# A two-layer attention kernel: softmax values and sums from one matrix product, quotients taken in transposed form

## The chip, the cores and the metric

The kernel runs on one core of one Trainium2 chip. The metric is device time in microseconds (us) of one execution. A core has a matrix engine (PE, TensorE), a vector engine (DVE), an activation engine (ACT), GpSimd (POOL) and DMA queues; most of the kernel's transfers are issued by SyncE (SP). PE writes only to PSUM, 8 banks of 2 KB in each of 128 partitions. Each engine executes its own instructions in program order and waits on semaphores that others raise.

## The reference, cut to what matters

Sixteen sequences of 256 tokens, model width 128, 16 heads of width 8, go through two layers, each `x = x + attention(norm(x)) * silu(feed_forward(norm(x)))`. The change touches attention alone:

```python
# layer 0 (full attention with a relative position bias)
scores = einsum('bhtd,bhsd->bhts', q, k) / sqrt(8) + rpe_bias
out = einsum('bhts,bhsd->bhtd', softmax(scores, -1), v)     # then heads side by side
s = out @ w_out + b_out

# layer 1 (causal)
attn = softmax(where(causal, q @ k.T / sqrt(8), -max), -1)
uniform = tril(ones / row)                                   # row = 1..256
new_attn = resid_gain * attn + skip_gain * eye - centre_gain * uniform
s = (new_attn @ v) @ cproj_w
```

The softmax of a row is computed as exponentials, their product with v ("values"), their sum ("sums"), and a quotient of the two.

## The kernel before

All is float32 but the scores' operands, which are split into three bfloat16 parts. Setup (to about 77 us) normalises, routes and builds tables; then comes attention of layer 0, the expert feed-forward and a middle part, and attention of layer 1. Expert and middle parts are not touched.

**Steps and units.** `attention()` is run once for each layer. Its work is a software pipeline over 16 batches (sequences): step k does pass A of batch k, pass B of batch k-1 and the end of batch k-2, and prepares q and k of batch k+1. Steps 3 to 14 are a hardware loop, the others are written out; layer 1's steps run from 0 to 17. Pass A computes scores with queries on the partitions and takes row maxima (DVE, L1178); pass B computes them transposed with the maximum subtracted, and takes exponentials (ACT, L1325 or L1330). A unit is 1024 columns of scores, that is two banks. There are 8 units a pass in layer 0 and 6 in layer 1, where the causal half is left out (units 0 to 3 have 256 columns a head, units 4 and 5 have 128). The class `Units` sets the order of a step, its positions numbered from 0:

```python
layer 0: A0 A1 A2 B0 A3 B1 A4 B2 A5 B3 A6 B4 A7 B5 B6 B7
layer 1: A0 A1 A2 B0 A3 B1 A4 B2 A5 B3 B4 B5
```

Six banks are a ring of three slots, one unit each: PE may write the unit at a position only when the unit three positions before has been read. In layer 0, DVE adds the position bias to each B unit (L1188) before ACT's exponential; in layer 1 ACT reads the ring itself.

**Values and sums.** `values()` (L1447) multiplies the exponentials of one unit by v: `vpad` holds v of each head in 8 of 32 columns, so that four heads fill the four 32-row strips of bank 6 (`od`), left half. In layer 0 the same routine then multiplies them by `onespad` for the sums, right half. In layer 1 POOL first adds units 4 and 5 onto units 0 to 3 (`add_tiles`, L1124), and PE takes sums of four units instead of six (`sums`, L1456). Units from `LATE` on (6 in layer 0, 2 in layer 1) are multiplied at the head of the next step, before A0 in layer 1 and after it in layer 0. `divide()` on DVE takes the reciprocal of the sums (L1198, 256 columns) and multiplies (L1203, L1205).

**Bank 7 (`misc`)** serves uses in a fixed order; `misc_free` makes each wait until the one before it in the list `MISC` has been read. They are QK (q and k of the next batch, L1464), V (v, L1487), in layer 1 E (the skip and centre products, L1493 and L1494), Y (output projection, L1503) and M (the maxima turned for pass B, L1517). `add_shape()` on DVE turns E into a running sum (L1213), weights it (L1216) and adds it to the quotient `on` (L1214, L1218). `project()` (L1244; L1249 and L1251) reads Y at the position `PROJECT`, the same at which PE computes Y.

**Operands of the scores.** ACT and POOL (in early steps of layer 0 DVE) split q and k (L1290 to L1301, L1111, L1116), SP writes the parts to DRAM (L1064) and loads them as `qs` and `ks` (L1071); A0 waits for these (16 x 2 loads of 384 KB).

## Time and profile before

| what | us |
|---|---|
| median of 3 runs | 1017.02 (1013.74 to 1020.98) |
| the profiled execution | 1019.83 |
| its span, first to last instruction | 1018.0 |
| PE busy | 853.4 (84%) |
| DVE busy | 729.1 (72%) |
| ACT busy | 455.0 (45%) |
| POOL busy | 336.7 (33%) |
| mean granted PE clock | 0.937 of full speed |

Layer 0's attention lies between about 78 and 490 us, layer 1's between about 717 us and the end. In a row of a timeline the first number is the start in us from the span's start, the second the time from the first start to the last end of `xcount` like instructions; a matrix product's row ends a little after the next one starts, because products are pipelined. A float32 product shows as two instructions. In brackets stands how long the engine had been idle and who released it.

### The profile page before, as it was taken

To read this page: it belongs to the slowest core of one execution; us is meant where nothing else is said; L and a number is where in the kernel's file an instruction comes from. 1 tells how busy PE (TensorE), PEld (TensorE's weight loads), DVE (VectorE), ACT (ScalarE), POOL (GpSimd) and SP (SyncE) were. 2 spreads that over 40 slices of the span, in tenths; PEclk is the share of its full clock that TensorE was granted. 3 is DMA by queue.
4 is the path that set the end of the run, shared out by engine and by line. 5 is a ranking of instruction groups with operands and counts; after the bars stand their busy time and mean duration, and the time that the engine had idled before them with its cause. 6 is when DMAs were issued, how large, how long until landed. Compare 5 with 4: busy or idle time off the path is not lost.

```text
span 1018.0 us, 21625 instructions
## 1 busy us (share of the span) xinstructions
PE 853.4 (84%) x7813; PEld 549.7 (54%) x7813; DVE 729.1 (72%) x1177; ACT 455.0 (45%) x809; POOL 336.7 (33%) x349
## 2 busy tenths in 40 slices
PE   0894785999999999999799999245689999999985
PEld 0742442555555555555366666234567666767763
DVE  5563784999999899997576767383557767676763
ACT  1252242454445444544344444277344545555532
POOL 7007773111111111100044444562135353434432
PEclk9996797999999999998799999757799999999999
DMA  5796441333332223223122222321543444444420
GB/s 138 227 156 162 118 110 34 79 74 73 85 68 63 63 63 78 63 48 126 33 67 66 67 67 66 101 83 46 110 100 87 109 95 102 87 110 94 99 44 11
DMA packets 105540, 88.37 MB, mean 87 GB/s; under 512 B 12565, under 2 KB 97497, under 8 KB 102409
## 3 DMA queue, kind: packets, MB, share of 16 engines
q1 hardware_dynamic: 96780, 76.54, 32.7%
q0 software_dynamic: 4352, 8.99, 2.9%
q10 hardware_dynamic: 4352, 2.10, 0.9%
q8 instruction: 35, 0.57, 0.2%
q14 instruction: 21, 0.17, 0.1%
HBM read 45.69 MB, written 41.11 MB: 85 GB/s over the span
## 4 chain that ended last, share of the span: by engine, by line
PE 19%; issue 13%; POOL 8%; DMA 4%; ACT 3%; DVE 3%; SPq 0%; POOLq 0%; ACTq 0%; DVEq 0%
PE ps L659 7%; POOL probs L1124 5%; PE ps L680 3%; DMA ks<-parts_d 3%; PE ps L661 2%; PE ps L671 2%; POOL qkr L1111 1%; POOL qk L1116 1%; ACT rows L875 1%; PE ps L653 1%; DMA parts_d<-qk 1%; PE ps L1398 1%; DMA probs<-mixed 1%; DVE mx L1178 0%; PE ps L912 0%
## 5 line engine op out<-in xcount | busy, mean ns | idle before, releaser
L1178 DVE TENSOR_REDUCE mx<-ps 128x4 f32<-128x1024 f32 (+1 forms) x224 | 269.9, 1218 | 100.4 <-PE ps L1398 67.3
L1325 ACT ACTIVATE probs<-probs 128x1024 f32<-128x1024 f32 x128 | 135.3, 1057 | 168.5 <-DVE probs L1188 166.0
L1188 DVE TENSOR_TENSOR probs<-ps,tabB 128x1024 f32<-128x1024 f32 x128 | 152.6, 1214 | 3.8 <-PE ps L1418 3.8
L1330 ACT ACTIVATE probs<-ps 128x1024 f32<-128x1024 f32 x96 | 96.5, 1023 | 97.0 <-PE ps L1456 39.4
L1447 PE MATMUL ps<-probs,vpad 128*32 128x256 f32 (+1 forms) x2048 | 131.6, 363 | 3.2 <-ACT probs L1325 1.2
L1390 PE MATMUL ps<-tabA,eyeb 128*128 128x512 bf16 x256 | 100.6, 393 | 29.8 <-DVE probs L1188 18.0
L1124 POOL TENSOR_TENSOR probs<-probs 128x512 f32<-128x512 f32 x64 | 78.9, 1264 | 136.1 <-PE ps L1447 136.1
L747 POOL DMA_INDIRECT mixed<-probs x72 | 69.7, 968 | 112.3 <-DVE probs L736 111.7
L1392 PE MATMUL ps<-ks,qs 96*128 96x256 bf16 x512 | 100.4, 277 | 0.0
L1418 PE MATMUL ps<-qs,ks 99*128 99x256 bf16 x512 | 76.2, 278 | 16.8 <-DVE mx L1178 11.4
L1198 DVE RECIPROCAL rden<-ps 128x256 f32<-128x256 f32 x32 | 56.2, 1756 | 36.5 <-PE ps L1456 24.8
L1447 PE MATMUL ps<-probs,onespad 128*32 128x256 f32 x1024 | 81.5, 391 | 0.0
L659 PE MATMUL ps<-qs,probs 128*128 x144 | 80.0, 638 | 0.0
L1447 PEld LDWEIGHTS ps<-probs,vpad 128*32 128x32 f32 x2048 | 53.5, 110 | 47.7 <-issue 17.9
L1111 POOL TENSOR_TENSOR qkr<-qkf,qk 128x512 f32<-128x512 f32 x28 | 32.3, 1154 | 126.7 <-ACT qk L1297 126.7
L1392 PEld LDWEIGHTS ps<-ks,qs 96*128 96x128 bf16 x512 | 51.5, 100 | 36.8 <-issue 3.6
L1152 POOL DMA_INDIRECT slots_in<-rows,place x64 | 62.3, 973 | 19.6 <-issue 18.9
L1418 PEld LDWEIGHTS ps<-qs,ks 99*128 99x128 bf16 x512 | 45.2, 98 | 42.2 <-DVE mx L1178 26.9
L718 DVE TENSOR_SCALAR probs<-ps 128x256 f32<-128x256 f32 x72 | 30.6, 425 | 49.5 <-PE ps L661 49.5
L700 ACT ACTIVATE probs<-ps 128x256 f32<-128x256 f32 x72 | 27.7, 385 | 78.9 <-PE ps L671 78.9
L1116 POOL TENSOR_TENSOR qk<-qkr,qk 128x512 bf16<-128x512 f32 x28 | 32.3, 1154 | 80.9 <-ACT qk L1301 80.9
L1390 PEld LDWEIGHTS ps<-tabA,eyeb 128*128 128x128 bf16 x256 | 25.7, 100 | 49.4 <-DVE probs L1188 26.4
(225 smaller groups left out, 1578.6 us busy)
## 6 DMA issues: line engine op xcount, KB each, us to landing
parts_d<-qk SPq DMA_DIRECT2D x64, 192.0 KB, 2.3
qs<-parts_d SPq DMA_DIRECT2D x32, 384.0 KB, 4.9
ks<-parts_d SPq DMA_DIRECT2D x32, 384.0 KB, 6.7
parts_d<-qk SPq DMA_DIRECT2D x64, 128.0 KB, 1.9
slots_in<-probs SPq DMA_DIRECT2D x1, 4680.0 KB
probs<-slots_in SPq DMA_DIRECT2D x72, 65.0 KB, 1.8
parts_d<-qk SPq DMA_DIRECT2D x64, 64.0 KB, 1.6
probs<-mixed SPq DMA_DIRECT2D x16, 256.0 KB, 3.3
```

The costliest lines, as they stand in the source:

```text
L659: nc.tensor.matmul(ps[:, b, :], xgT[:, b, :], wgu[:, bass.ds(e, 1), :].rearrange("p a n -> p (a n)"), start=True, stop=False)
L747: nc.gpsimd.indirect_dma_start(v.mixed[:, :], bass.IndirectOffsetOnAxis(ap=rows[:, b:b + 1], axis=0), yo[:, b % 4, :], None).then_inc(y_st ...
L1124: nc.gpsimd.tensor_tensor(later, later, second, ALU.add).then_inc(added, 1)
L1152: nc.gpsimd.indirect_dma_start(v.slots_in[:, :], bass.IndirectOffsetOnAxis(ap=v.place[:, k, t:t + 1], axis=0), v.rows[:, t, :], None).then ...
L1178: nc.vector.tensor_reduce(mx[:, s.buf(), t, heads[0]:heads[-1] + 1], ring[:, slot].rearrange("p (h n) -> p h n", n=w), AX.X, ALU.max).then ...
L1188: nc.vector.tensor_tensor(probs[:, j, :].rearrange("p (h n) -> p h n", n=T), ring[:, slot].rearrange("p (h n) -> p h n", n=T), v.tabB[:, h ...
L1325: nc.scalar.activation(probs[:, j, :], probs[:, j, :], ACT.Exp).then_inc(exp_done, 1)
L1330: nc.scalar.activation(probs[:, j, :], ring[:, slot], ACT.Exp).then_inc(exp_done, 1)
L1390: nc.tensor.matmul(o[:, T * n:T * n + 2 * T], eyeb[:], v.tabA[:, h:h + 2, off:off + T], start=True, stop=False, skip_group_check=True)
L1392: mm = nc.tensor.matmul(at, q, ks[0:MROW, b, h, :], start=False, stop=True, skip_group_check=True)
L1418: mm = nc.tensor.matmul(at, k, qs[0:MROW + PARTS, b, h, :], start=(n % 2 == 0), stop=True, skip_group_check=True)
L1447: mm = nc.tensor.matmul(od[32 * q:32 * q + 32, T * what + t0:T * what + T], lhs, probs[:, j, w * n:w * n + w], start=(j == 0 and what == 0 ...
```

## The change

Values and sums come from one product: `vpad` now has v in 8 columns, ones in the next 8 and zeros in 16, and a head's 32 columns are taken from a place that puts values and sums of two groups of heads above each other in a strip, in the left or right half of `od`. `add_tiles` and `sums` are gone, and so is `onespad`. At position 0 of a step (layer 1) or 1 (layer 0) ACT copies `od` to SBUF (`copy_products`), PE turns it so that tokens are on the partitions (`tokens_apart`, use T of bank 7), DVE takes reciprocals of 32 columns and multiplies (`divide`), and PE turns the result back (`heads_apart`, use N): in layer 0 by two transposes and a copy by ACT (`quotients`, at position `BACK`), in layer 1 by adding it as a product into the bank that holds the skip product. The residual gain moves into v's weights. The order of bank 7 becomes QK, T, N, Y, V, M. The diff, with setup's edits cut:

```diff
-        v.vpad = sb("vpad", [P, 3, 8, 160])
-        v.onespad = sb("onespad", [P, 4, 32])
+        v.vpad = sb("vpad", [P, 3, 8, 128])
...
     LATE = 2 if layer else 6
-    PROJECT = 10 if layer else 11
-    GROUPS = 4
+    APART, DIVIDE, BACK, PROJECT, VALUE = (3, 2, 6, 8, 10) if layer else (4, 5, 7, 9, 12)
+    PROJECTED = PROJECT + 1
...
-    MISC = ["QK", "V", "E", "Y", "M"] if layer else ["QK", "V", "Y", "M"]
+    MISC = ["QK", "T", "N", "Y", "V", "M"]
...
             def divide(s):
-                if layer == 0:
-                    dve.wait_ge(pv_done, NU * (s.n(-2) + 1))
-                else:
-                    dve.wait_ge(sum_done, GROUPS * (s.n(-2) + 1))
-                nc.vector.reciprocal(rden[:], od[:, T:2 * T]).then_inc(rd_done, 1)
+                dve.wait_ge(apart_full, s.n(-2) + 1)
...
+                turned = misc.rearrange("p (g e d) -> p g e d", e=2, d=HD)
+                nc.vector.reciprocal(rden[:], turned[:, :, 1, 0]).then_inc(rd_done, 1)
                 dve.wait_ge(rd_done, s.n(-2) + 1)
...
+                nc.vector.tensor_tensor(onT[:].rearrange("p (g d) -> p g d", d=HD), turned[:, :, 0, :],
+                                        rden[:].unsqueeze(2).broadcast_to([P, 2 * H, HD]), ALU.mult).then_inc(apart_done, 1)
+
+            def add_shape(s):
+                n = 2 * s.n(-2)
+                dve.wait_ge(e_full, s.n(-2) + 1)
+                nc.vector.tensor_tensor_scan(cum[:], v.onesT[:], misc[:, T:2 * T], 0.0, ALU.mult, ALU.add).then_inc(e_evac, 1)
+                dve.wait_ge(e_evac, n + 1)
+                nc.vector.tensor_tensor(cum[:], cum[:], v.share, ALU.mult).then_inc(shaped, 1)
+                dve.wait_ge(shaped, s.n(-2) + 1)
...
+                nc.vector.tensor_tensor(on[:], misc[:, 0:T], cum[:], ALU.add).then_inc(e_evac, 1)
...
                 for pos, (kind, j) in enumerate(U.order):
-                    if layer == 0 and pos == 1 and s.has(-2):
+                    if pos == DIVIDE and s.has(-2):
                         divide(s)
                     if U.exists(s.k, kind):
                         (maximum if kind == "A" else add_bias if layer == 0 else lambda *a: None)(s, j, U.slot(s.k, pos))
                     if kind == "A" and j == NU - 1 and s.has() and (layer or s.k < LOOP):
                         maximum_parts(s)
-                    if layer and pos == 4 and s.has(-2):
-                        divide(s)
-                    if layer and pos == 7 and s.has(-2):
+                    if layer and pos == BACK and s.has(-2):
                         add_shape(s)
...
-                    if pos == PROJECT and s.has(-2):
+                    if pos == PROJECTED and s.has(-2):
                         project(s)
...
+            def copy_products(s):
+                act.wait_ge(pv_done, NU * (s.n(-2) + 1))
...
+                nc.scalar.activation(ods[:].rearrange("p r t -> p (r t)"), od, ACT.Copy).then_inc(od_copied, 1)
+
+            def quotients(s):
+                act.wait_ge(back_full, s.n(-2) + 1)
...
+                nc.scalar.activation(on[:], misc[:, 0:T], ACT.Copy).then_inc(on_done, 1)
...
-                for what in range(2 if layer == 0 else 1):
-                    for n, h in enumerate(heads):
-                        i, q = h // 4, h % 4
-                        lhs = vpad[:, b, 4 * c + q, 32 * i:32 * i + 32] if what == 0 else onespad[:, i, :]
-                        mm = nc.tensor.matmul(od[32 * q:32 * q + 32, T * what + t0:T * what + T], lhs,
...
+                for n, h in enumerate(heads):
+                    i, q = h // 4, h % 4
+                    r, first_column = i % 2, 32 * i - 16 * (i // 2)
+                    mm = nc.tensor.matmul(od[32 * q:32 * q + 32, T * r + t0:T * r + T],
+                                          vpad[:, b, 4 * c + q, first_column:first_column + 32],
...
+            def tokens_apart(s):
+                misc_free(pe, s, "T")
+                pe.wait_ge(od_copied, s.n(-2) + 1)
+                for c in range(2):
+                    for r in range(2):
+                        at = 2 * P * c + P * r
+                        mm = nc.tensor.transpose(misc[:, at:at + P], ods[:, r, P * c:P * c + P], eye)
+                mm.then_inc(apart_full, 1)
+
+            def heads_apart(s):
+                misc_free(pe, s, "N")
+                if layer == 0:
+                    pe.wait_ge(apart_done, s.n(-2) + 1)
+                    for c in range(2):
+                        mm = nc.tensor.transpose(misc[:, P * c:P * c + P], onT[:, P * c:P * c + P], eye)
+                    mm.then_inc(back_full, 1)
+                else:
+                    nc.tensor.matmul(misc[:, T:2 * T], v.wv1[:, 1, :], batch_tokens(s, -2), start=True, stop=True,
+                                     skip_group_check=True)
+                    nc.tensor.matmul(misc[:, 0:T], v.wvs[:], batch_tokens(s, -2), start=False, stop=False, skip_group_check=True)
+                    pe.wait_ge(apart_done, s.n(-2) + 1)
+                    for c in range(2):
+                        mm = nc.tensor.matmul(misc[:, P * c:P * c + P], onT[:, P * c:P * c + P], eye, start=False, stop=True,
+                                              skip_group_check=True)
+                    mm.then_inc(e_full, 1)
...
+                    if pos == PROJECT and s.has(-2):
+                        misc_free(pe, s, "Y")
+                        if layer:
+                            pe.wait_ge(e_evac, 2 * (s.n(-2) + 1))
+                        else:
+                            pe.wait_ge(on_done, s.n(-2) + 1)
...
-                    if pos == 4 and s.has():
+                    if pos == VALUE and s.has():
                         misc_free(pe, s, "V")
```

What this does to the order of PE in layer 1 (a step of the hardware loop; `wo,on` is the output projection Y, `maskA` and `ks,qs` with 128x512 and 128x128 are unit A5 or A4, `maskB` with 128x2x128 is a B unit, `probs,vpad` are values 0 and 1). Before:

```order
L1401 MATMUL ps<-maskA,eyeb 128x512
L1403 MATMUL ps<-ks,qs 128x128 x4
L1401 MATMUL ps<-maskA,eyeb 128x512
L1403 MATMUL ps<-ks,qs 128x128 x4
L1374 REGISTER_ALU
L1422 MATMUL ps<-maskB,eyeb 128x2x128
L1424 MATMUL ps<-qs,ks 128x256 x2
L1422 MATMUL ps<-maskB,eyeb 128x2x128
L1424 MATMUL ps<-qs,ks 128x256 x2
L1447 MATMUL ps<-probs,vpad 32x256 x8
L1503 MATMUL ps<-wo,on 128x128 x2
L1427 MATMUL ps<-maskB,eyeb 128x512
```

This is A5, B3, values 0 and 1, and only then Y. With the change the same engine has, from A4 on:

```order
L1413 MATMUL ps<-maskA,eyeb 128x512
L1415 MATMUL ps<-ks,qs 128x128 x4
L1413 MATMUL ps<-maskA,eyeb 128x512
L1415 MATMUL ps<-ks,qs 128x128 x4
L1386 REGISTER_ALU
L1434 MATMUL ps<-maskB,eyeb 128x2x128
L1436 MATMUL ps<-qs,ks 128x256 x2
L1434 MATMUL ps<-maskB,eyeb 128x2x128
L1436 MATMUL ps<-qs,ks 128x256 x2
L1525 MATMUL ps<-wo,on 128x128 x2
L1413 MATMUL ps<-maskA,eyeb 128x512
L1415 MATMUL ps<-ks,qs 128x128 x4
```

Y now stands behind A4 and B2 and ahead of A5. On DVE in layer 1, `add_shape` of before, between the maxima of A4 and A5:

```order
L1178 TENSOR_REDUCE mx<-ps 128x8 [waits l1_a_full]
L1213 SCALAR_TENSOR_TENSOR cum<-onesT,ps 128x256 [waits l1_on,l1_e_full]
L1214 TENSOR_TENSOR on<-ps,on 128x256
L1215 ISA
L1216 TENSOR_TENSOR cum<-cum,cst 128x256 [waits l1_e_evac]
L1217 REGISTER_ALU
L1218 TENSOR_TENSOR on<-on,cum 128x256 [waits l1_shaped]
```

and the same place with the change:

```order
L1179 TENSOR_REDUCE mx<-ps 128x8 [waits l1_a_full]
L1208 SCALAR_TENSOR_TENSOR cum<-onesT,ps 128x256 [waits l1_e_full]
L1209 ISA
L1210 TENSOR_TENSOR cum<-cum,cst 128x256 [waits l1_e_evac]
L1214 TENSOR_TENSOR on<-ps,cum 128x256 [waits l1_y_full,l1_shaped]
```

One addition is gone; the group still stands behind the maximum of A4. On DVE in layer 0, the head of a step before (B5 to B7, A0, divide, A1, A2, B0):

```order
L1188 TENSOR_TENSOR probs<-ps,tabB 128x1024 [waits l0_pv_done,l0_b_full] x3
L1177 ISA
L1178 TENSOR_REDUCE mx<-ps 128x4 [waits l0_a_full]
L1198 RECIPROCAL rden<-ps 128x256 [waits l0_pv_done]
L1203 TENSOR_TENSOR on<-ps,rden 128x256 [waits l0_y_full,l0_rd]
L1177 REGISTER_ALU
L1178 TENSOR_REDUCE mx<-ps 128x4 [waits l0_a_full]
```

and with the change (A0, A1, A2, B0, A3, divide, B1):

```order
L1179 TENSOR_REDUCE mx<-ps 128x4 [waits l0_a_full]
L1178 REGISTER_ALU
L1179 TENSOR_REDUCE mx<-ps 128x4 [waits l0_a_full]
L1178 REGISTER_ALU
L1179 TENSOR_REDUCE mx<-ps 128x4 [waits l0_a_full]
L1189 TENSOR_TENSOR probs<-ps,tabB 128x1024 [waits l0_pv_done,l0_b_full]
L1178 REGISTER_ALU
L1179 TENSOR_REDUCE mx<-ps 128x4 [waits l0_a_full]
L1199 RECIPROCAL rden<-ps 128x32 [waits l0_back_full,l0_apart_full]
L1201 TENSOR_TENSOR onT<-ps,rden 128x256 [waits l0_rd]
L1189 TENSOR_TENSOR probs<-ps,tabB 128x1024 [waits l0_pv_done,l0_b_full]
```

The division has moved from behind A0 to behind A3.

## Rows read from the trace of the kernel before

**Rows 1.** Timeline of DVE, layer 0, one step from A0's maximum on

```profile
240.74 1.23 DVE L1178 TENSOR_REDUCE mx<-ps 128x4 f32<-128x1024 f32 x1 [1.05 <-PE ps L1392]
242.63 1.76 DVE L1198 RECIPROCAL rden<-ps 128x256 f32<-128x256 f32 x1 [0.67 <-PE ps L1447]
...
244.86 2.35 DVE L1178 TENSOR_REDUCE mx<-ps 128x4 f32<-128x1024 f32 x2
...
263.54 1.22 DVE L1178 TENSOR_REDUCE mx<-ps 128x4 f32<-128x1024 f32 x1 [1.05 <-PE ps L1392]
```

**Rows 2.** Timelines of PE and ACT at the head of that step

```profile
242.50 1.13 PE L1464 MATMUL ps<-xnT,wqk 128*128 x4
243.46 0.38 PE L1390 MATMUL ps<-tabA,eyeb 128*128 128x512 bf16 x1
...
237.46 3.32 ACT L1325 ACTIVATE probs<-probs 128x1024 f32<-128x1024 f32 x3 [1.54 <-DVE probs L1188]
```

**Rows 3.** Timeline of PE, layer 1, one step from A0 to the next A0

```profile
886.81 0.28 PE L1396 MATMUL ps<-maskA,eyeb 128*128 128x256 bf16 x1 [0.35 <-DMA ks<-parts_d]
...
887.49 1.03 PE L1464 MATMUL ps<-xnT,wqk 128*128 x4
...
890.34 0.61 PE L1487 MATMUL ps<-wv,xb 128*128 128x128 f32 x4
...
891.54 1.93 PE L1456 MATMUL ps<-probs,onespad 128*32 128x256 f32 x32
...
894.08 0.38 PE L1401 MATMUL ps<-maskA,eyeb 128*128 128x512 bf16 x1
...
894.97 0.65 PE L1493 MATMUL ps<-xnT,wvs 128*128 x2
...
904.03 0.28 PE L1396 MATMUL ps<-maskA,eyeb 128*128 128x256 bf16 x1 [0.43 <-DMA ks<-parts_d]
```

**Rows 4.** Lines of layer 1's division over the whole trace: DVE timeline, first and eleventh

```profile
752.85 1.76 DVE L1198 RECIPROCAL rden<-ps 128x256 f32<-128x256 f32 x1 [0.67 <-PE ps L1456]
...
928.08 1.76 DVE L1198 RECIPROCAL rden<-ps 128x256 f32<-128x256 f32 x1 [0.67 <-PE ps L1456]
```

**Rows 5.** Small operations of the kinds added: reciprocal (DVE, setup), transposes (PE, experts)

```profile
75.89 0.35 DVE L339 RECIPROCAL wt<-probs 128x32 f32<-128x32 f32 x1
...
561.75 0.38 PE L671 MATMUL ps<-cst,probs 128*128 128x128 f32 x2
```

**Rows 6.** Timeline of DVE in the step of rows 3: `add_shape`, maxima's parts, `project`

```profile
896.87 0.68 DVE L1213 TENSOR_TENSOR_SCAN cum<-onesT,ps 128x256 f32<-128x256 f32 x1
...
897.89 0.42 DVE L1216 TENSOR_TENSOR cum<-cum,cst 128x256 f32<-128x256 f32 x1
898.35 0.42 DVE L1218 TENSOR_TENSOR on<-on,cum 128x256 f32<-128x256 f32 x1
...
899.94 0.18 DVE L1227 CAST m<-mx 128x32 bf16<-128x32 f32 x1
...
900.80 0.42 DVE L1249 TENSOR_TENSOR yt<-ps,rows 128x256 f32<-128x256 f32 x1
```

**Rows 7.** Last step of layer 1: timelines of PE (values, first sums) and DVE

```profile
1002.34 1.94 PE L1447 MATMUL ps<-probs,vpad 128*32 128x256 f32 x48
1005.27 0.64 PE L1456 MATMUL ps<-probs,onespad 128*32 128x256 f32 x8 [0.99 <-POOL probs L1124]
...
1012.04 0.69 DVE L1213 TENSOR_TENSOR_SCAN cum<-onesT,ps 128x256 f32<-128x256 f32 x1
```

**Rows 8.** Early step of layer 1: PE timeline; windows (busy per engine, granted clock 0.67, DMA)

```profile
744.46 0.28 PE L1396 MATMUL ps<-maskA,eyeb 128*128 128x256 bf16 x1 [2.00 <-DMA ks<-parts_d]
...
749.64 0.61 PE L1487 MATMUL ps<-wv,xb 128*128 128x128 f32 x4
...
744.40:747.80 3.40, 3.34 (x17) 2.46 (x18) 1.22 (x1) 1.07 (x3) 2.66 (x3) 0.67 0.00 0
```

**Rows 9.** Timeline of POOL, layer 1, the step of rows 3: the last part of q and k

```profile
893.87 1.15 POOL L1116 TENSOR_TENSOR qk<-qkr,qk 128x512 bf16<-128x512 f32 x1 [1.67 <-ACT qk L1301]
```

More of the change, by code:

```diff
@@ L65 @@
 C_ALL = C_SPARE + FLIGHT
-W_LOADS, R_LOADS = 14, 5
+W_LOADS, R_LOADS = 16, 5
 PAIR_OF_MINUS_ONES = float.fromhex("-0x1.017f00p+0")
@@ L522, in _ @@
                     mm.then_inc(lg, 1)
-            pe.wait_ge(copied, 4 + 4 + 13)
-            for k in range(6):
+            pe.wait_ge(copied, 4 + 4 + 15)
+            for k in range(5):
                 nc.tensor.matmul(ps[:, 2, k:k + 1], rowsp[:, k, :], v.ones[0:1, 0:1], start=True, stop=True)
@@ L1157, in body @@
             def body(s):
-                if layer and s.has(-2):
-                    for g in range(GROUPS):
-                        add_tiles(pool, s, g)
                 if s.has(1) and (layer or s.k >= LOOP):
@@ L1346, in body @@
                 for pos, (kind, j) in enumerate(U.order):
+                    if pos == (0 if layer else 1) and s.has(-2):
+                        copy_products(s)
+                    if layer == 0 and pos == BACK and s.has(-2):
+                        quotients(s)
+                    if pos == VALUE and s.has():
+                        values(s)
                     if kind == "B" and U.exists(s.k, kind):
@@ L1450, in values @@
-                mm.then_inc(pv_done, 1)
-            def sums(s, g):
-                pe.wait_ge(added, GROUPS * s.n(-2) + g + 1)
-                for q in range(4):
-                    mm = nc.tensor.matmul(od[32 * q:32 * q + 32, T:2 * T], onespad[:, g, :], probs[:, g, T * q:T * q + T],
-                                          start=False, stop=(g == GROUPS - 1), skip_group_check=True)
-                mm.then_inc(sum_done, 1)
+                for n, h in enumerate(heads):
[3 more added lines that the diff above has]
+                                          vpad[:, b, 4 * c + q, first_column:first_column + 32],
+                                          probs[:, j, w * n:w * n + w], start=(j == 0 and i == 0),
+                                          stop=(j == NU - 1), skip_group_check=True)
@@ L1481, in body @@
                         projections(s)
-                    if pos == 4 and s.has():
+                    if pos == APART and s.has(-2):
+                        tokens_apart(s)
+                    if pos == BACK and s.has(-2):
+                        heads_apart(s)
+                    if pos == PROJECT and s.has(-2):
[4 more added lines that the diff above has]
+                            pe.wait_ge(on_done, s.n(-2) + 1)
+                        for c in range(2):
+                            mm = nc.tensor.matmul(misc[:, D * c:D * c + D], on[:, P * c:P * c + P], wo[:],
+                                                  start=True, stop=True)
+                        mm.then_inc(y_full, 1)
+                    if pos == VALUE and s.has():
                         misc_free(pe, s, "V")
@@ L1510, in body @@
                         values(s, -1, j - 2)
-                    if layer and pos == 4 and s.has(-2):
-                        for g in range(GROUPS):
-                            sums(s, g)
                 if s.has():
```

117 lines of the change are left out of this document (47 added, 70 removed).

## The prediction

> **What bounds the kernel now.** I read first the busy times, which name PE, and then one steady step of each layer in the timelines, since the two layers have different limits.
>
> In layer 0 a step takes 22.80 us, from one maximum of A0 to the next [rows 1]. Sixteen passes of DVE over 1024 columns (two of them start 1.13 apart: 2.35 us for both) make 18.1 of these. The division takes 2.23, from 242.63 to 244.86, and the projection's addition some 0.35. The rest, about 2.1, is waiting, most of it at the step's head: 1.05 before A0's maximum and 0.67 before the division. So DVE bounds layer 0, and the head of a step, where PE and ACT finish the batch before, adds to it.
>
> In layer 1 a step is 17.22 us from A0 to A0 [rows 3], on the mean of ten steps 17.52 ((928.08 - 752.85) / 10) [rows 4]. PE is idle in it for 0.43 us only, before A0, and waits there for the load of `ks`. So layer 1 is bound by PE, with the way of q and k through DRAM just behind: from the end of POOL's last part at 895.02 [rows 9] to A0 at 904.03 it is 9.0 us. In these rows a product's entry runs 0.16 past the start of the next, and the engine that reads it starts 0.2 after that start; I use 0.2 for each handover from PE and 0.05 for the others.
>
> **Layer 1, what is saved.** The sums cost PE 1.9 us a step [rows 3]; they go, and values and sums come at the price of values alone, as the same 32 columns are loaded and the same columns streamed. POOL's additions go as well, so the parts of q and k are ready earlier. Added to PE: four transposes of 128 columns and two float32 products of 128. The transposes: two took 0.38 with 0.16 of overlap, so 0.11 each and 0.45 for four [rows 5]. The products: V is the same pair, 0.61 - 0.16 = 0.45 [rows 3]. PE's work is 17.22 - 0.43 = 16.8 before and 16.8 - 1.9 + 0.45 + 0.45 = 15.8 after. If nothing else waited, a step would gain 1 us.
>
> The Trainium skill (TensorE: Matmul & The Clock Gate, Part 4: PE-mode transpose) gives about 275 ns for a 128x128 transpose in one kernel's context. By it four would take 1.1 and not 0.45, and a step 0.65 more. The row shows 0.38 for two, so back to back they are cheaper, and the sum goes by the row.
>
> **Layer 1, what waits.** The new positions put three waits on PE, which executes in order. I follow a step from A0 = 0, with 0.68 for a unit of 256-column heads (886.81 to 887.49), 0.86 for QK and 0.89 for A4 and A5 (894.08 to 894.97) [rows 3].
>
> 1. B1 writes the slot of A2. `divide` now stands on DVE ahead of A2's maximum. PE: A0 to 0.68, QK to 1.54, A1 and A2 to 2.9, transposes to 3.35, B0 and A3 to 4.7. DVE: A1's maximum 2.4 to 3.55, reciprocal of 32 columns 0.35 (setup has this very shape [rows 5], where 256 columns took 1.76), product 0.42 [rows 6], A2's maximum from 4.3 on, finished at 5.5. PE waits 0.85.
> 2. Y is computed at position 8 and needs `on`. Behind the end of A4's product comes 0.2, its maximum 1.13, the scan 0.68, then 0.03, the weighting 0.42, 0.04, the last addition 0.42 and 0.05 [rows 6]: 2.97 in all. PE has only B2 in between, 0.67. It waits 2.3. Before, Y stood behind A5, B3 and values 0 and 1 as well, which covered the same chain. Behind the waiting Y stands everything: A5, B3, the values; DVE itself runs dry, since A5's maximum is its next work.
> 3. V is at position 10 and its bank is free when `project` has read Y. DVE gets there from Y's start after Y 0.45, A5 0.89, 0.2, A5's maximum 1.25, the four operations on the maxima 0.86 (899.94 to 900.80), the product and its signal 0.47 [rows 6]: 4.1. PE has Y, A5, B3 and values 0 and 1 (half of what four sums cost, 0.95, with a gap of 0.1): 3.1. It waits 1.0.
>
> A step is then 15.8 + 0.85 + 2.3 + 1.0 = 19.95, against 17.52 on the mean, 2.45 more. Steps 2 to 15 have all three parts: 14 x 2.45 = +34. ACT's new copy (512 columns, 0.6 as about half an exponential over 1024, three of which take 3.32 [rows 2]) lies beside A0 and QK and is done 2 us before the transposes; without that cover each 0.1 would cost as much. The load of `ks` is no longer late: q and k are ready at about 7 (B0's product 4.0, exponential 1.1, ACT's part 0.6, POOL's 1.15), plus 9.0 is 16, and A0 comes at 19.9.
>
> **Layer 1, its end.** The last step has no units. Before, from the end of the values at 1004.28 to the scan at 1012.04 it was 7.75 us, with PE waiting for POOL's additions [rows 7]. Now the way is copy 0.2 + 0.6, transposes 0.15 + 0.45, reciprocal and product 0.2 + 0.8, skip and centre products with the quotients 0.05 + 1.35, and 0.2: 4.0. With one addition less behind the scan (0.35) this gives -4.1. Step 16 has no A units either and loses part of its wait for POOL: -1.3. Together -5.4.
>
> **Layer 0.** At the head, unit 5's values and sums take 0.45 less, so A0's maximum can begin at 240.3. The three last exponentials end at 240.78 all the same [rows 2], because DVE's additions feed them; then values 7 (0.05 + 0.45), QK 0.96 (242.50 to 243.46), A1 0.89 (as many columns as A4 of layer 1) and 0.2 bring A1's maximum to 243.3, where it was 244.86: -1.55. The long reciprocal had stood in this gap and was largely covered by it. The new division costs DVE 0.75 in the middle, where DVE has no gap. V at position 12 waits for the projection's addition behind A6 and then delays A7: project's start + 0.4 + V 0.45 + A7 0.89 + 0.2 is 1.9, while DVE has 1.45 of work: +0.5. Net -0.3 to -0.2 a step, 13 steps: -3. In step 2 the projection's addition also waits until POOL's scatter for the expert part has landed; it now has one more B unit behind it, +1.1, one pass of DVE [rows 1]. Together -2. The reciprocal's 1.4 us a step thus brings almost nothing.
>
> **The clock.** In an early step PE had been idle for 2.00 us, and the next stretch has a mean granted clock of 0.67, that is in part the lower level of 1.2 GHz [rows 8]. From A0 to V it took 5.18 us there (744.46 to 749.64) and 3.53 in the steady step (886.81 to 890.34) [rows 3]: 1.65 lost. The wait at Y is longer than that 2.00, but it is followed by work that is partly covered by the wait at V. I count half of the 14 steps at 1.0: +7, with bounds of 0 and 14 x 1.65 = 23.
>
> **The sum**, against the profiled execution's own 1019.8: +34 - 5.4 - 2 + 7 = +33.6, so 1053.4. Setup changes by a few short operations beside idle stretches, under 0.5. The profiled execution is 2.8 above the median of the runs shown; against the median the sum gives 1050.6. I forecast 1052.
>
> Bounds: the three waits may be each off by 0.2 or 0.3 from handovers, -0.7 to +0.7 a step, -10 to +10. A transpose by the row of a product pair rather than back to back (0.38 for two without overlap) gives +0.3 a step, +4. The product with the broadcast reciprocal has no row; it lies between 0.35 and 1.22 (DVE's pass over 1024 columns), and I take 0.42, the row of 256 columns; at the upper end +0.8 on the first wait and in each step of layer 0, +20, which no row supports.
>
> **Rivals.**
> *The clock falls in every step* (0.16). For it: each step now has a wait longer than that of [rows 8], and the other two beside it. Against: it has more work around it. 14 x 1.65 instead of 7 gives +16: 1068. Beside it stands the Trainium skill (the same page, A second HAM failure mode: psum-queue depth-cycling), which reports a clock that oscillates with frequent short idle times of PE; no steady step shows that here, the clock in these stays at 2.4 GHz with PE waits of 0.4.
> *Layer 0 gains its head in full* (0.12): A7 is not delayed and the new division falls into a gap. Then 13 x 1.3 more: 1038.
> *Layer 0 loses* (0.08): PE does some 3 us less there in about the same step, in short pieces, and the clock falls there too, 13 x 1: 1065.
> *The other side, not slower* (0.06): the wait at Y does not arise, because DVE's chain behind A4 is done before PE has written B2. Then V's wait shrinks too, and the way of q and k decides: 7 + 9.0 = 16.0 a step, 14 x -1.5 = -21, and with the end and layer 0 about 992. It turns at one number: A4's product to the last addition must take less than 0.67, where the rows add up to 2.97. It could come about only if DVE had no maximum to take first.
>
> **How the numbers follow.** The forecast's own case has 0.58, the rivals 0.16, 0.12, 0.08 and 0.06. Its own range is 1041 to 1064. For 8 in 10 I reach down to the full gain of layer 0 and up to the clock in every step: 1036 to 1072. Faster by over 1% (about what a measurement of this kernel can tell from none): the last rival, 0.05. Within 1%: what lies between it and the rest, 0.04. Slower by over 1%: 0.91.
>
> **What would show it.** In layer 1's steady step: PE idle before Y by about 2.3 with DVE as releaser, before V by about 1.0, before B1 by 0.85; no wait for `ks`; a period near 20. In layer 0: a DVE wait of about 1.9 before A1's maximum, about 0.5 before A7's, a period near 22.6. In the last step 4 us from values to scan. I am wrong if layer 1's period is under 18.5 or PE does not wait at Y; only mis-sized if the waits are there and the clock differs.

## The result, and the profile after

| | before | after |
|---|---|---|
| median of the runs | 1017.99 us (1013.74 to 1020.98, 4 runs) | 1055.18 us (1051.31 to 1063.01, 4 runs) |
| profiled execution: time, span | 1019.8, 1018.0 us | 1051.31, 1049.5 us |
| ratio of the times | 1 | 1.0378, 95% interval 1.0304 to 1.0453 |

The change makes the kernel 37 us slower; 1052 was forecast, with a range of 1036 to 1072. The busy times of the page for the kernel after:

```profile
PE 805.7 (77%) x6484; PEld 531.1 (51%) x6499; DVE 681.6 (65%) x1164; ACT 479.3 (46%) x857; POOL 258.8 (25%) x282
```

No engine is close to full, and yet the kernel is slower: waits were added, not work. Below are the waits of PE from 720 us on: which products waited and for what, then the us in total, how often, and the longest. Before, PE waited in most steps of layer 1 only for `ks`, 0.4 in the step of [rows 3] and 1.3 at most between 760 and 1000 us.

```profile
PE ps L1525 <- DVE on L1214: 34.5, 16, 2.3
PE ps L1533 <- DVE yt L1245: 12.5, 14, 1.0
PE ps L1434 <- DVE mx L1179: 11.1, 14, 1.0
PE ps L1408 <- DMA ks<-parts_d: 2.2, 1, 2.2
```

L1525 is the projection Y, L1533 the value projection V, L1434 the first product of B1. The load of `ks` makes PE wait once, in an early step. The same three in the timeline of PE for one step, A0 to A0, which answers to [rows 3]:

```profile
904.61 0.28 PE L1408 MATMUL ps<-maskA,eyeb 128*128 128x256 bf16 x1
...
907.47 0.60 PE L1471 MATMUL ps<-cst,ods 128*128 128x128 f32 x4
907.91 0.27 PE L1434 MATMUL ps<-maskB,eyeb 128*128 128x256 bf16 x1
...
910.14 0.28 PE L1434 MATMUL ps<-maskB,eyeb 128*128 128x256 bf16 x1 [0.74 <-DVE mx L1179]
...
910.81 0.60 PE L1483 MATMUL ps<-xnT,wv 128*128 x2
...
912.12 0.38 PE L1413 MATMUL ps<-maskA,eyeb 128*128 128x512 bf16 x1
912.34 0.39 PE L1415 MATMUL ps<-ks,qs 96*128 96x128 bf16 x4
...
916.09 0.68 PE L1525 MATMUL ps<-wo,on 128*128 128x128 f32 x4 [2.26 <-DVE on L1214]
...
920.29 0.71 PE L1533 MATMUL ps<-wv,xb 128*128 128x128 f32 x4 [0.96 <-DVE yt L1245]
```

The next A0 begins at 924.64. And DVE in that step, for [rows 6]:

```profile
908.15 0.35 DVE L1199 RECIPROCAL rden<-ps 128x32 f32<-128x32 f32 x1
908.53 0.42 DVE L1201 TENSOR_TENSOR onT<-ps,rden 128x256 f32<-128x256 f32 x1
908.87 2.35 DVE L1179 TENSOR_REDUCE mx<-ps 128x4 f32<-128x1024 f32 x2
913.21 1.23 DVE L1179 TENSOR_REDUCE mx<-ps 128x8 f32<-128x1024 f32 x1 [1.99 <-PE ps L1415]
914.35 0.68 DVE L1208 TENSOR_TENSOR_SCAN cum<-onesT,ps 128x256 f32<-128x256 f32 x1
...
915.52 0.42 DVE L1214 TENSOR_TENSOR on<-ps,cum 128x256 f32<-128x256 f32 x1
917.70 1.23 DVE L1179 TENSOR_REDUCE mx<-ps 128x8 f32<-128x1024 f32 x1 [1.75 <-PE ps L1415]
```

The two engines stand still in turn. DVE waits 1.99 for A4's product; then PE waits 2.26 for what DVE does behind A4's maximum; then DVE waits 1.75 for A5, which stands behind Y on PE.

Where the 31.5 us between the spans went can be read from the starts of A0's maximum in steps 2 and 15 of layer 1. Before these are 745.33 and 974.48, after 742.29 and 1007.05. Up to step 2 of layer 1 the kernel after gains 3.04. Of these 2.65 are there already in step 2 of layer 0, where an addition waits for the landing of a scatter: it starts at 161.41 instead of 164.06 (the last section has more on it). The 13 steps between take 264.76 instead of 229.15, which is +35.6. From step 15 to the end of the span it is 42.4 instead of 43.5, so -1.1: step 15 loses as the others do, and the end is shorter.

The reciprocals of layer 1 start at 764.95, 785.14, 805.17, 825.24, 846.64 and so on: steps of 20.03 to 20.19, and in every third one 21.4, on the mean of eleven 20.43 ((989.69 - 764.95) / 11), where [rows 4] gave 17.52. What the longer ones have is in the timeline of PE behind Y of such a step:

```profile
894.71 1.19 PE L1525 MATMUL ps<-wo,on 128*128 128x128 f32 x4 [2.25 <-DVE on L1214]
895.69 0.63 PE L1413 MATMUL ps<-maskA,eyeb 128*128 128x512 bf16 x1
896.12 0.63 PE L1415 MATMUL ps<-ks,qs 96*128 96x128 bf16 x4
```

The first product of A5 takes 896.12 - 895.69 = 0.43; the same one of A4 above takes 912.34 - 912.12 = 0.22. The clock is at the lower of its two levels (1.2 instead of 2.4 GHz) from 894.4 to 897.8, as the granted clock of that window shows (the number behind the instruction counts, as a share of full speed):

```profile
894.40:897.80 3.40, 3.10 (x16) 2.41 (x17) 0.32 (x2) 0.00 (x0) 0.00 (x0) 0.51 0.90 145
```

So it falls 0.3 before the wait of 2.25 is over, and the work behind the wait runs at half the clock.

In layer 0 the timeline of DVE, which answers to [rows 1]:

```profile
239.37 1.22 DVE L1179 TENSOR_REDUCE mx<-ps 128x4 f32<-128x1024 f32 x1 [0.72 <-PE ps L1404]
242.41 2.36 DVE L1179 TENSOR_REDUCE mx<-ps 128x4 f32<-128x1024 f32 x2 [1.82 <-PE ps L1404]
...
246.94 0.35 DVE L1199 RECIPROCAL rden<-ps 128x32 f32<-128x32 f32 x1
...
256.76 1.22 DVE L1179 TENSOR_REDUCE mx<-ps 128x4 f32<-128x1024 f32 x1 [0.55 <-PE ps L1404]
257.90 3.48 DVE L1189 TENSOR_TENSOR probs<-ps,tabB 128x1024 f32<-128x1024 f32 x3
262.00 1.23 DVE L1179 TENSOR_REDUCE mx<-ps 128x4 f32<-128x1024 f32 x1 [0.62 <-PE ps L1404]
```

Over nine steps the period is 22.73 ((383.31 - 178.76) / 9), and 22.74 before ((379.08 - 174.39) / 9, from the reciprocals of that trace). The granted clock between 180 and 380 us is 1.00 in both. Layer 0's steady steps give nothing.

The last step, PE and in the last row DVE, for [rows 7]:

```profile
1037.94 1.94 PE L1458 MATMUL ps<-probs,vpad 128*32 128x256 f32 x48
1040.70 0.63 PE L1471 MATMUL ps<-cst,ods 128*128 128x128 f32 x4 [0.81 <-ACT ods L1331]
...
1043.20 0.61 PE L1488 MATMUL ps<-cst,onT 128*128 128x128 f32 x4
...
1043.85 0.69 DVE L1208 TENSOR_TENSOR_SCAN cum<-onesT,ps 128x256 f32<-128x256 f32 x1 [1.67 <-PE ps L1488]
```

The scan starts 3.97 behind the end of the values at 1039.88. Before, these were 7.76.

### The profile page after: what moved, and what is told of

It reads as the page before. It is cut to its first block, busy times and chain, and to the rows that moved or that the text cites. A ratio compares the mean times of both kernels' runs of the same rounds, so it can differ in the third digit from the quotient of the medians.

```text
span 1049.5 us, 18980 instructions
## 1 busy us (share of the span) xinstructions
PE 805.7 (77%) x6484; PEld 531.1 (51%) x6499; DVE 681.6 (65%) x1164; ACT 479.3 (46%) x857; POOL 258.8 (25%) x282
## 4 chain that ended last, share of the span: by engine, by line
PE 33%; DVE 10%; issue 4%; DMA 3%; ACT 3%; POOL 1%; SPq 0%; DVEq 0%; ACTq 0%
PE ps L671 7%; DVE mx L1179 4%; PE ps L692 3%; PE ps L1458 3%; PE ps L683 2%; PE ps L1410 2%; PE ps L1415 1%; PE ps L1413 1%; DMA ks<-parts_d 1%; PE ps L1441 1%; PE ps L1525 1%; ACT rows L887 1%; PE ps L673 1%; PE ps L1439 1%; PE ps L1496 1%
## 5 line engine op out<-in xcount | busy, mean ns | idle before, releaser
L1458 PE MATMUL ps<-probs,vpad 128*32 128x256 f32 (+1 forms) x2048 | 125.8, 365 | 11.6 <-ACT probs L1319 11.5
L1402 PE MATMUL ps<-tabA,eyeb 128*128 128x512 bf16 x256 | 103.0, 402 | 23.3 <-DMA ks<-parts_d 11.8
L1404 PE MATMUL ps<-ks,qs 96*128 96x256 bf16 x512 | 103.1, 284 | 0.0
L730 DVE TENSOR_SCALAR probs<-ps 128x256 f32<-128x256 f32 x72 | 30.6, 425 | 49.0 <-PE ps L673 35.6
L1430 PEld LDWEIGHTS ps<-qs,ks 99*128 99x128 bf16 x512 | 48.3, 100 | 21.0 <-issue 6.6
L1525 PE MATMUL ps<-wo,on 128*128 128x128 f32 x128 | 25.1, 326 | 41.3 <-DVE on L1214 34.5
L1533 PE MATMUL ps<-wv,xb 128*128 128x128 f32 x128 | 23.0, 304 | 40.1 <-DVE rows L1240 27.6
L1410 PE MATMUL ps<-ks,qs 96*128 96x256 bf16 x256 | 47.2, 281 | 0.0
```

Source lines behind the costliest of these rows:

```text
L1402: nc.tensor.matmul(o[:, T * n:T * n + 2 * T], eyeb[:], v.tabA[:, h:h + 2, off:off + T], start=True, stop=False, skip_group_check=True)
L1404: mm = nc.tensor.matmul(at, q, ks[0:MROW, b, h, :], start=False, stop=True, skip_group_check=True)
L1410: mm = nc.tensor.matmul(at, q, ks[0:MROW, b, h, :], start=False, stop=True, skip_group_check=True)
L1430: mm = nc.tensor.matmul(at, k, qs[0:MROW + PARTS, b, h, :], start=(n % 2 == 0), stop=True, skip_group_check=True)
L1458: mm = nc.tensor.matmul(od[32 * q:32 * q + 32, T * r + t0:T * r + T], vpad[:, b, 4 * c + q, first_column:first_column + 32], probs[:, j, w ...
```

## The experiments

The theory is that PE's three waits make the difference in layer 1, and that they come from the places of the new parts and not from the parts. The rivals are the merged product and its float32 operations themselves, the way of q and k, and the clock. All times are medians. The kernel before had 1017.6 to 1022.0 beside them, and a ratio is always to the kernel before on the same chip.

| kernel | us | ratio, 95% interval | layer 1's step | clock, 760 to 1000 us |
|---|---|---|---|---|
| before | 1018 | | 17.5 | 1.00 |
| after | 1055.2 | 1.0378 (1.0304 to 1.0453) | 20.43 | 0.98 |
| e1, division later | 1054.2 | 1.0366 (1.0297 to 1.0436) | 20.34 | 0.94 |
| e2, scan ahead | 1020.3 | 1.0012 (0.9978 to 1.0045) | 18.05 | 1.00 |
| e3, Y and V later | 1011.1 | 0.9943 (0.9914 to 0.9972) | 17.41 | 1.00 |
| e4, all places | 992.3 | 0.9745 (0.9674 to 0.9815) | 16.02 | 0.99 |
| e9, e1 with the wait filled | 1045.7 | 1.0251 (1.0206 to 1.0296) | 19.55 | 1.00 |
| e5, short reciprocal | 1010.8 | 0.9929 (0.9897 to 0.9961) | 17.44 | 0.99 |
| e6, no sums | 988.5 | 0.9678 (0.9631 to 0.9725) | 16.05 | 0.99 |
| e7, V later in layer 0 | 1052.6 | 1.0305 (1.0237 to 1.0374) | 20.62 | 0.94 |
| e10, after again | 1056.6 | 1.0359 (1.0297 to 1.0421) | 20.77 | 0.93 |
| e8, e4 and e7 | 983.1 | 0.9635 (0.9589 to 0.9681) | 16.11 | 0.97 |

The steps are means of eleven, from the reciprocal of step 3 to that of step 14. The clock is the mean granted clock as a share of full speed. In e4, e6 and e8 that window takes in the layer's last steps, and what they miss to 1.00 lies behind 960 us.

**e1: the division behind A2's maximum.**

```diff
-    APART, DIVIDE, BACK, PROJECT, VALUE = (3, 2, 6, 8, 10) if layer else (4, 5, 7, 9, 12)
+    APART, DIVIDE, BACK, PROJECT, VALUE = (3, 3, 6, 8, 10) if layer else (4, 5, 7, 9, 12)
```

> In layer 1 the reciprocal and the product go behind A2's maximum instead of ahead of it; nothing else is changed. Theory (the three waits of PE add up, since PE executes in order and is busy between them): B1's wait of 0.74 goes, the waits at Y (2.26) and V (0.96) stay as they are, a step falls from 20.03 to 19.3 and the time by 14 x 0.74 = 10 us, to about 1041 where the changed kernel has 1051. Rival (the step is set by the load of q and k or by the DVE chain as a whole, PE's waits only fill it up): what B1 no longer waits is waited at Y or before A0, the step stays at 20.0 and the time at 1051.

Measured 1054.2, which can't be told from the kernel after. The theory's 1041 is missed; the rival is near in time, but not for its reason: the list of waits has the 2.26 at Y as before and none for `ks`. The wait at B1 is gone, and four steps of eleven are shorter, 19.55 to 19.58. That is 0.48 saved and not 0.74, since B1 and the skip product still start 0.18 and 0.14 later than they would back to back. But the other seven take 20.6 to 20.9. The window 760 to 1000 of e1 (busy us and instructions by engine, then the granted clock):

```profile
760.00:1000.00 240.00, 204.53 (x2087) 152.46 (x2079) 129.11 (x198) 111.43 (x177) 27.73 (x24) 0.94 0.40 87
```

The granted clock is 0.94 there. In these steps the row of Y is followed by products at 1.2 GHz:

```profile
913.69 1.20 PE L1525 MATMUL ps<-wo,on 128*128 128x128 f32 x4 [2.26 <-DVE on L1214]
914.68 0.63 PE L1413 MATMUL ps<-maskA,eyeb 128*128 128x512 bf16 x1
```

So there is a third account besides the waits' sum and the way of q and k: the clock took back what the wait gave. The next experiment tests it.

**e9: e1, with PE kept busy in Y's wait.**

```diff
+                        for _ in range(2 if layer and U.exists(s.k, kind) else 0):
+                            first_pass(s, pos, j, again=True)
                         misc_free(pe, s, "Y")
```

> e1 again, and in layer 1 PE computes A5's scores twice more (2 x 0.89 = 1.78 us of work whose result is overwritten) before it waits for Y, in the middle of the wait of 2.26. What is computed in the end is the same. Theory (in e1 what the wait at B1 gave back went to stretches at the lower clock, which follow the idle 2.26): PE is idle for 0.5 only, no stretch at the lower clock is left, every step is 19.55 as the undisturbed steps of e1 are, on the mean 0.8 less, so 14 x 0.8 = 11 us faster than e1, about 1043, with more work on PE. Rival 1 (the longer steps of e1 come from the order itself, the clock is by the way): the extra work is hidden at best, 1054, steps of 20.9 stay. Rival 2 (the extra work isn't hidden): 14 x 1.8 more, 1079.

Measured 1045.7: 8.5 less than e1 with 1.8 us more work for PE in each step. The two ran on different chips, and their ratios to the kernel before, 1.0251 and 1.0366, have intervals that just don't meet. The four runs lie within 2.5 us (1044.25 to 1046.76), those of e1 within 8.9. The window and the waits of PE in it:

```profile
760.00:1000.00 240.00, 221.65 (x2441) 166.58 (x2442) 131.69 (x208) 117.32 (x187) 27.72 (x24) 1.00 0.41 87
```

```profile
PE ps L1535 <- DVE yt L1245: 12.5, 13, 1.0
PE ps L1527 <- DVE on L1214: 5.8, 12, 0.5
```

Y's wait is 0.5 long, the clock is 1.00, and every step from step 3 on takes 19.53 to 19.57. Nothing else was changed, so the idle time at Y is what brings the clock down, and without it e1's own gain shows: 19.55 against the 20.03 of the kernel after. V waits 0.96 here too, and the clock stays up.

**e2: the scan ahead of A4's maximum.**

```diff
+                    if layer and pos == BACK and s.has(-2):
+                        add_shape(s)
                     if U.exists(s.k, kind):
                         (maximum if kind == "A" else add_bias if layer == 0 else lambda *a: None)(s, j, U.slot(s.k, pos))
...
-                    if layer and pos == BACK and s.has(-2):
-                        add_shape(s)
```

> In layer 1 the scan and the two operations behind it go ahead of A4's maximum instead of behind it. Theory: the way from the end of the skip product to the last addition is then 0.2 + 0.68 + 0.03 + 0.42 + 0.04 + 0.42 + 0.05 = 1.84, and PE has A4 (0.89) and B2 (0.67) in it: Y waits 0.3 instead of 2.26. V waits some 0.3 longer, since A5's maximum comes later on DVE. A step of about 18.1, 14 x 2.0 = -28 us, so about 1024, and less by up to 4 if the stretches at the lower clock go with the long wait. Rival 1 (the wait moves to V in full, because project stays behind A5's maximum): step 20. Rival 2 (no stretches at the lower clock change): 1024 and every third step still 1.4 longer.

Measured 1020.3. The step is 18.05, the wait at Y some 0.24 (3.1 in 13 steps), at V 0.96 (it was thought 0.3 longer, and isn't), at B1 0.79; every step lies between 17.97 and 18.16, and none has a stretch at the lower clock any more. Two lines of order on DVE, with no change to PE's program, are worth 35 us. Of the 2.38 that a step is shorter, 1.98 are Y's wait (20.03 - 18.05), and the other 0.40 are the clock. In the waits of PE from 760 to 1000:

```profile
PE ps L1533 <- DVE yt L1245: 12.5, 13, 1.0
PE ps L1434 <- DVE mx L1179: 10.3, 13, 1.0
PE ps L1525 <- DVE on L1214: 3.1, 13, 0.2
```

**e3: Y at position 10, V at 11.**

```diff
-    APART, DIVIDE, BACK, PROJECT, VALUE = (3, 2, 6, 8, 10) if layer else (4, 5, 7, 9, 12)
+    APART, DIVIDE, BACK, PROJECT, VALUE = (3, 2, 6, 10, 11) if layer else (4, 5, 7, 9, 12)
```

> In layer 1 the projection moves from position 8 to 10 and the value projection from 10 to 11, so that A5, B3 and values 0 and 1 stand between the skip product and Y. Theory: Y's wait of 2.26 goes in full, B1's 0.74 stays, V's stays at about 1.0 (the projection's product stands behind A5's maximum and its four small operations): a step of 17.5, as long as before the change, 14 x -2.5 = -35 us less the clock's 4: about 1013, no difference from the kernel before that a run can tell. Rival (the merged product itself and its ten more float32 operations cost the time, not the order): step stays above 19, time over 1040.

Measured 1011.1, a step of 17.41. The wait at Y is gone from the steady steps and V's is 0.5, where 1.0 was expected. The merged product isn't dear: with the two projections moved back the changed kernel is 0.6% faster than the one before, where the rival had over 1040. The rival falls.

**e4: layer 1 in the order that leaves no wait.** `add_shape` as in e2, and

```diff
-    APART, DIVIDE, BACK, PROJECT, VALUE = (3, 2, 6, 8, 10) if layer else (4, 5, 7, 9, 12)
-    PROJECTED = PROJECT + 1
+    APART, DIVIDE, BACK, PROJECT, VALUE = (5, 6, 8, 11, 10) if layer else (4, 5, 7, 9, 12)
+    PROJECTED = PROJECT if layer else PROJECT + 1
...
-    MISC = ["QK", "T", "N", "Y", "V", "M"]
+    MISC = ["QK", "T", "N", "V", "Y", "M"] if layer else ["QK", "T", "N", "Y", "V", "M"]
```

> The same arithmetic as the changed kernel, layer 1 in another order: transposes at position 5, division at 6 ahead of A4's maximum, skip and quotient products at 8, the scan ahead of A5's maximum, the value projection at 10 and the projection at 11 (bank order QK, T, N, V, Y, M). Theory: none of the three waits arises, PE's work is 15.8 a step and the way of q and k through DRAM (7 + 9.0 from A0) is just behind it: a step of 16.0, 14 x -1.5 against the kernel before, with the shorter end -5: about 990. The clock stays at its full level in every step. Rival (the change's own work is dearer than 15.8 when packed): step 17.5, time 1015. Rival 2 (another wait, of the exponentials or of the bank, takes the place): step 17 to 18.

Measured 992.3, 2.5% faster than before (1.9 to 3.3). The step is 16.02, with steps of 15.86 among them, and between 829 and 847 us, which is longer than a step, the timeline of PE shows no wait. So the 15.86 is also a measurement of the 15.8 which the prediction gave for PE's work, added operations included.

**e6: what the change removes, alone.**

```diff
-                        for g in range(GROUPS):
-                            sums(s, g)
...
-                    for g in range(GROUPS):
-                        add_tiles(pool, s, g)
...
-                nc.vector.reciprocal(rden[:], od[:, T:2 * T]).then_inc(rd_done, 1)
+                nc.vector.reciprocal(rden[:], od[:, 0:T] if layer else od[:, T:2 * T]).then_inc(rd_done, 1)
```

> The kernel before; in layer 1 the sums (16 products a step) and POOL's four additions are left out, and the reciprocal reads the values instead, so layer 1's quotients are others. It is what the change removes, with nothing added and no place moved. Theory: PE's work is 14.9 a step, the way of q and k (7 + 9.0) bounds, a step of 16.0 instead of 17.5: 14 x -1.5 = -21, the last two steps lose their wait for POOL, -5, about 992; PE waits some 1.1 for ks before A0. Rival (the full 1.9 counts, since POOL's additions also stood before q and k's parts): a step of 15.4, about 985. Rival 2 (ks bounds already before): 17.4, about 1013.

Measured 988.5, a step of 16.05. The number is as expected, the mechanism is not: PE waits for `ks` in one step of the window only (0.8). Instead it waits 0.43 at B3 for A4's maximum, since DVE, with the long reciprocal in its way, comes late to it:

```profile
PE ps L1416 <- DVE mx L1175: 6.0, 14, 0.5
...
PE ps L1390 <- DMA ks<-parts_d: 0.8, 1, 0.8
```

So the bound of 16.0 by the way of q and k was too long, and by its first part: in such a step POOL's last part ends at 832.91, 6.5 behind A0 at 826.41 and not 7, and the next A0 comes 9.3 later, at 842.25, without a wait. The 9.0 is not refuted by this. The removed work is worth some 30 us (1018 - 988.5). What was added, and where it was put, cost 67 on top of that, and e4 gets 63 of these back by order alone.

**e5: layer 0's reciprocal over 32 columns, in the kernel before.**

```diff
-                nc.vector.reciprocal(rden[:], od[:, T:2 * T]).then_inc(rd_done, 1)
+                some = 2 * H if layer == 0 else T
+                nc.vector.reciprocal(rden[:, 0:some], od[:, T:T + some]).then_inc(rd_done, 1)
```

> The kernel before; in layer 0 alone the reciprocal takes 32 columns instead of 256, and the product uses them broadcast over 8 columns each, so layer 0's quotients are others. Theory (the reciprocal stands in the gap that PE leaves at a step's head): A1's product ends at 244.34 in that step, its maximum can begin 0.2 later, 244.54, where it begins at 244.86; so of the 1.41 us saved only 0.3 count, 14 steps: -4 us, about 1014, and DVE waits 1.1 for PE before A1's maximum. Rival (DVE bounds layer 0, so its work counts in full): 14 x -1.4 = -20, about 999.

Measured 1010.8, 7 less, with an interval of 4 to 10. The steps of layer 0 are 22.49 instead of 22.74, so 3.5 of it is there; the rest I can't place. DVE in a step:

```profile
243.92 0.36 DVE L1199 RECIPROCAL rden<-ps 128x32 f32<-128x32 f32 x1 [0.67 <-PE ps L1449]
244.41 0.42 DVE L1204 TENSOR_TENSOR on<-ps,rden 128x256 f32<-128x256 f32 x1
245.83 2.36 DVE L1178 TENSOR_REDUCE mx<-ps 128x4 f32<-128x1024 f32 x2 [1.00 <-PE ps L1394]
```

Most of the 1.4 saved is turned into a wait of 1.00 for PE. The reciprocal, the longest of the small operations, was covered by the gap it stood in: by its duration it would be worth 20 us, by the steps it is worth 3.5, and by the times at most 10.

**e7: V behind A7 in layer 0.** In the changed kernel the layer 0 positions become `(4, 5, 7, 9, 14)`.

> The changed kernel; in layer 0 alone the value projection moves from position 12 to 14, behind A7. Theory (V's wait for the projection's addition delays A7 by 0.55): DVE's wait before A7's maximum goes, a step of layer 0 falls from 22.73 to 22.2 and the time by 13 x 0.55 = 7 us, to about 1045 to 1047. Rival (the head of the next step is set by PE and ACT and takes it back, as the values of V come later): a step stays at 22.7, 1053.

Measured 1052.6 (1044.28 to 1055.35), where the theory had 1045 to 1047 and the rival 1053. The rival falls all the same, since it had a step of 22.7. Layer 0 did what the theory says: no wait before A7's maximum, a step of 22.14 on the mean of nine ((383.98 - 184.68) / 9). But layer 1, whose code is the same as in the kernel after, took 20.62 a step at a clock of 0.94, and in step 2 of layer 0 the addition that waits for the scatter started at 167.05 instead of 161.41. The 7.7 us (13 steps of 0.59) are there in layer 0, and the total hides them.

**e10: the changed kernel again.**

> The changed kernel once more, unchanged, to see what varies from execution to execution. In e7 layer 1 was the same code as in the changed kernel, but its steps took 20.62 on the mean and not 20.39. Theory 1 (which steps fall to the lower clock is not set by the code): steps of 20.03 and longer ones mixed otherwise than in the first execution, a mean between 20.0 and 20.8; the scatter that the projection's addition in step 2 waits for lands somewhere between 161 and 167, and moves the rest by as much. Theory 2 (it is set by the code): steps of 20.03 with every third 21.40, as before. Time 1050 to 1057 by both.

Measured 1056.6. Theory 1 holds. Layer 1's steps are 20.06 to 21.99, on the mean 20.77, and the window has

```profile
760.00:1000.00 240.00, 202.65 (x2078) 149.80 (x2071) 126.44 (x196) 111.98 (x179) 27.41 (x24) 0.93 0.37 82
```

against a clock of 0.98 in the first execution. Which steps fall to the lower clock is not set by the code: 12 of the 14 do here and 4 did in the first execution. Nor is the place in the step where it falls, and that sets the price. In this step the clock is down from 903.1 to 906.5, when Y and most of A5 are done:

```profile
901.81 0.68 PE L1525 MATMUL ps<-wo,on 128*128 128x128 f32 x4 [2.26 <-DVE on L1214]
...
906.56 0.71 PE L1533 MATMUL ps<-wv,xb 128*128 128x128 f32 x4
```

V no longer waits, so its 0.96 has taken up part of the loss, and the step is 20.6. Where the clock fell ahead of Y, at 894.4 in the first execution, A5 was late and with it DVE's chain, V still waited 0.81, and the step was 21.4.

**e8: e4's layer 1 and e7's layer 0 together**, the positions `(5, 6, 8, 11, 10)` and `(4, 5, 7, 9, 14)`.

> e4 in layer 1 and e7 in layer 0 together. Theory: layer 1 takes 16.0 a step and layer 0 22.14 instead of 22.73: 13 x 0.59 = 7.7 us less than e4's 992, about 985, and layer 1 keeps its full clock since PE waits for nothing in it. Rival (the two do not add up, since layer 0's end or the expert part between takes the gain back): 992.

Measured 983.1 (979.77 to 985.46, 6 runs), 3.65% faster than before and 7.0% faster than the change as it was given (983.1 / 1056.6, e10 on the same chip). The step of layer 0 is 22.15, so the gain of e7, which its own total hid, adds to that of e4. The same instructions as in the kernel after, in another order:

```profile
PE 799.4 (81%) x6484; PEld 526.9 (54%) x6499; DVE 679.7 (69%) x1164; ACT 478.7 (49%) x857; POOL 258.7 (26%) x282
```

## Why the prediction was right

- *PE's work in layer 1, 15.8.* Right: e4's shorter steps take 15.86. The four transposes take 907.91 - 907.47 = 0.44 for the 0.45 said, the skip, centre and quotient products 912.12 - 910.81 = 1.31 for the 1.35 said, the broadcast product on DVE 0.42 (a price without a row, taken from the nearest). The Trainium skill's 275 ns for a transpose (TensorE: Matmul & The Clock Gate, Part 4: PE-mode transpose) is not what four in a row take here, 0.11 each.
- *The three waits.* The profile has 0.74, 2.26 and 0.96, for 0.85, 2.3 and 1.0. It counts from the end of an entry, which runs 0.16 past the next start; counted from where the product would start back to back, as the prediction did, they are 0.90, 2.42 and 1.12. An undisturbed step is 20.03, for 19.95. (19.95 less 17.52 is 2.43 and not 2.45, and 14 of either make 34.) e2, e3 and e4 show that they are causes: each shrinks when its place is changed, and the step with it, to 18.05, 17.41 and 16.02 for 18.1, 17.5 and 16.0 expected.
- *The load of q and k no longer late.* Right: A0 doesn't wait for it in a steady step. But it was also thought the next bound at 16.0, and e4 and e6 have steps of 15.86 and 15.84 in which A0 doesn't wait for it either.
- *The clock, +7.* The term was near in size in the profiled execution, and that was luck: seven steps at 1.0 were counted, and there were four at 1.37 (21.40 - 20.03), which is 5.5. Nothing in the rows of before could say how many there would be. In e10 the mean step is 20.77, so it is 14 x 0.74 = 10. The rival "the clock falls in every step" is thus nearly what another execution of the same kernel does, only at half its price; the two belong together as one term that varies. What the Trainium skill reports of a clock that oscillates with frequent short idle times of PE (the same page, A second HAM failure mode: psum-queue depth-cycling) these executions show in a like form, with 2.26 idle at Y in each step and a mean clock of 0.93 to 0.98, where no steady step of the kernel before did.
- *Layer 1's end, -5.4.* The last step's 3.97 is the 4.0 said. From step 15 on the sum is -1.1. With about +2.5 in it for that step's waits and +1.4 for its stretch at the lower clock, the end is -5.0.
- *Layer 0, -2.* Each part was near: head -1.41 in the step shown (1.05 - 0.72 of A0's wait, and 3.04 instead of 4.12 from A0's to A1's maximum) for -1.55; division +0.72 for +0.75; A7 +0.55 for +0.5. Their sum is -0.1 and the mean over nine steps 0, for -0.2 to -0.3. That the time up to layer 1's step 2 came out at -3.04, near the -2, is luck: 2.65 of it is the scatter's earlier landing. e5 confirms the step behind it (the reciprocal stood in a gap), e7 the wait before A7.
- *The sum.* 34 for the waits, -5.0, -3.0 and 5.5 make 31.5, the difference of the spans, for +33.6. The recorded 1038 of the rival "Layer 0 gains its head in full" doesn't follow from its own 13 x 1.3, which gives 1035.
- *The rivals.* "Layer 0 gains its head in full" is what layer 0 does in e7, but for 7.7 us and not 17, as the division still costs its 0.75 in the middle. "Layer 0 loses" is refuted by its clock of 1.00. "Not slower, because Y's wait doesn't arise" was refused on the sum 2.97 against 0.67; measured from the end of A4's product at 913.01 to Y at 916.09 it is 3.08.

What the prediction had no eye for is that waits and clock are not independent: its sum values the removal of B1's wait at 10 us or more, and e1 gave none that the times show.

## What to carry to other kernels

Before a merge of operations is judged by the work that it saves, follow each new chain between two engines that execute in order, and count what stands between the producer and the consumer on the consumer's engine: here two lines of order on DVE were worth 35 us, and all the removed work 30. A maximum ahead of a short chain that another engine waits for costs that engine the maximum's duration and the product that the maximum itself waits for: 2.0 a step in e2, 1.13 of DVE and 0.89 of PE. If a small repair brings nothing, look at the granted clock before the theory is given up, and test by filling the wait. Filling is the test and not the cure: e9 is at 1045.7, and e2 and e4, which remove the wait, are at 1020.3 and 992.3.
